# Four edits at the seams of a four-layer cross-attention kernel: interleaved row maxima, re-spread loads, an on-chip copy of Q rows, and sums of two tiles on TensorE

## The reference, cut to what matters

```python
q = hidden_states @ Wq                       # 2048 x 1024, 16 heads of 64
k = encoder_hidden_states @ Wk               # 1601 x 1024
v = encoder_hidden_states @ Wv
logits = jnp.einsum('bhqd,bhkd->bhqk', q, k) * scale
logits = logits + col_bias[None, None, :, :] # two masked columns pairs get -20
probs = jax.nn.softmax(logits, axis=-1)
out = jnp.einsum('bhqk,bhkd->bhqd', probs, v)
out = out @ Wo + bo + residual
```

## Time and profile before

| quantity | value |
|---|---|
| time, three runs | 4746.79, 4748.32, 4752.88 us; median 4748.32 us |
| time of the profiled execution | 4749.55 us, of which its span is 4747.40 us (2.15 us lie around the span) |
| busy share of the span | PE 97%, PEld 60%, DVE 67%, ACT 48%, POOL 55% |
| mean granted TensorE clock | 0.983 of full speed |
| Q phases | about 503 to 604 us, 2469 to 2543 us, 3603 to 3676 us |

### The profile page before, as it was taken

One profiled execution on the slowest core, in us unless ns is written; L12 is line 12 of the kernel. 1 busy time (PEld: TensorE's weight loads), 2 busy tenths in 40 slices (PEclk: granted clock), 3 DMA queues, 4 the chain that ended last, 5 costly groups with the idle time before them and its releaser, 6 DMA issues.

```text
span 4747.4 us, 55870 instructions
## 1 busy us (share of the span) xinstructions
PE 4584.1 (97%) x20473; PEld 2827.9 (60%) x20473; DVE 3192.8 (67%) x5093; ACT 2296.7 (48%) x4069; POOL 2621.8 (55%) x1266
## 2 busy tenths in 40 slices
PE   8999799999999989999989999999998999999999
PEld 7888565555555445555546655555555655555554
DVE  3321367777777778887846777777766777777777
ACT  3232355454444436666664555445454544454543
POOL 0000267887778500110126777887774777887775
PEclk9999899999999979999999999999999999999999
DMA  4564822221221021011134122211216122221210
GB/s 155 165 208 153 273 61 56 57 58 33 57 58 42 3 51 22 19 24 27 23 99 149 44 52 58 58 42 40 57 46 199 33 55 58 58 57 34 57 42 19
DMA packets 99522, 332.29 MB, mean 70 GB/s; under 512 B 13797, under 2 KB 32229, under 8 KB 87274
## 3 DMA queue, kind: packets, MB, share of 16 engines
q1 hardware_dynamic: 99248, 328.71, 25.5%
HBM read 193.15 MB, written 120.31 MB: 66 GB/s over the span
## 4 chain that ended last, share of the span: by engine, by line
PE 89%; DVE 6%; issue 3%; DMA 1%; ACT 1%; POOL 0%; SPq 0%; DVEq 0%; ACTq 0%
PE ST L890 13%; PE SS L871 12%; PE ST L891 12%; PE OA L901 12%; PE OB L901 11%; PE ST L1003 4%; PE OA L1011 4%; PE SS L922 4%; PE SS L989 3%; DVE mpart L1494 2%; PE SS L911 2%; DVE R L1510 1%; PE OB L989 1%; PE ST L937 1%; PE ST L939 1%
## 5 line engine op out<-in xcount | busy, mean ns | idle before, releaser
L774 POOL TENSOR_TENSOR acc<-acc,P 128x1024 f32<-128x1024 f32 x900 | 2153.6, 2424 | 617.7 <-DVE acc L1426 604.5
L1190 ACT ACTIVATE P<-ST 128x512 f32<-128x512 f32 (+1 forms) x2496 | 1465.5, 597 | 1297.8 <-PE ST L891 1150.3
L1402 DVE TENSOR_REDUCE mpart<-SS 128x1 f32<-128x400 f32 (+1 forms) x3072 | 1627.8, 569 | 640.7 <-PE SS L871 562.9
L871 PE MATMUL SS<-KS,QS 68*128 68x400 f32 (+1 forms) x3072 | 1042.7, 373 | 43.0 <-DMA QS<-q_parts 29.8
L890 PE MATMUL ST<-QX,KX 128*128 128x512 f32 (+1 forms) x2496 | 1033.1, 414 | 1.9 <-ACT stw L1097 1.8
L891 PE MATMUL ST<-QS,KS 69*128 69x512 f32 (+1 forms) x2496 | 989.2, 396 | 0.0
L871 PEld LDWEIGHTS SS<-KS,QS 68*128 68x128 f32 x3072 | 585.1, 191 | 260.2 <-DVE mpart L1402 52.9
L890 PEld LDWEIGHTS ST<-QX,KX 128*128 128x128 f32 (+1 forms) x2496 | 463.0, 185 | 387.9 <-issue 284.8
L901 PE MATMUL OA<-P,Vp 128*64 128x512 f32 (+1 forms) x2496 | 658.3, 606 | 0.0
L901 PE MATMUL OB<-P,Vp 128*64 128x512 f32 (+1 forms) x2496 | 641.3, 592 | 0.0
L1261 ACT ACTIVATE PG<-ST 128x512 f32<-128x512 f32 (+1 forms) x832 | 429.3, 614 | 245.6 <-PE ST L1003 245.3
(11 more groups left out here) (232 smaller groups left out, 4355.7 us busy)
## 6 DMA issues: line engine op xcount, KB each, us to landing
q_parts<-stq SPq DMA_DIRECT2D x96, 512.0 KB, 3.8
QX<-q_parts SPq DMA_DIRECT2D x96, 512.0 KB, 11.5
KX<-k_parts SPq DMA_DIRECT2D x48, 801.0 KB, 9.1
QS<-q_parts SPq DMA_DIRECT2D x48, 512.0 KB
v_tiles<-sv SPq DMA_DIRECT2D x24, 832.0 KB, 6.4
Vp<-v_tiles SPq DMA_DIRECT2D x24, 832.0 KB, 7.2
k_parts<-skh SPq DMA_DIRECT2D x48, 400.5 KB, 4.7
k_parts<-skl SPq DMA_DIRECT2D x48, 400.5 KB, 5.9
```

The source lines that it names most:

```text
L774: gp.tensor_tensor(out, out, P[0:k, slot(H, t), q, :], ALU.add).then_inc(pool_a, 1)
L871: pe.matmul(SS[at % 3][:, 0:w], QS[H % 3][0:SROWS, qt * 128:(qt + 1) * 128], KS[H % 3][0:SROWS, o:o + w], start=True, stop=True).then_inc( ...
L1190: act.activation(P[0:k, slot(H, t), j, :], ST[n % 3][0:k, :], ACT.Exp, scale=SCALE).then_inc(act_p, 1)
L1402: dve.tensor_reduce(mpart[H % 2][:, i // len(KCH), c:c + 1], SS[RING_AT["s", H, i] % 3][:, 0:w], AX.X, ALU.max).then_inc(dve_ss, 1)
```

## The change

Line numbers in the profile of before are those of before; the order listings below of the change carry its own.

1. `S_FROM, S_TO` go from 10, 26 to 8, 24, so `ROW_ITEM` goes from 27 to 25. Two of an item's four score tiles are issued between its two halves (`ct` = 0 and 1) and two behind it, no longer all four behind it.
2. The loads that SyncE issued in one block before the first Q phase (`first_loads`) are spread between the Q stores or moved behind them. The loads of `wqh` and `wql` are issued two K projections earlier. At the start of the first Q phase TensorE waits for each bank by itself.
3. QS of the first head is no longer read back from `q_parts`: after each of the first four stores SyncE copies the 64 rows from `stq` to `QS`, inside SBUF, in pieces of 512 queries.
4. In head 15 VectorE adds tiles 1, 2, 5 to 10, GpSimd tiles 3 and 4, and `sums` takes tiles 11 and 12 straight from P with eight more matmuls by ones. `sums` of head 15 is issued before the last `values`, and ScalarE's `take_z` before its `take_o`.

```diff
-S_FROM, S_TO = 10, 26
+S_FROM, S_TO = 8, 24
...
 def dve_tiles(h):
-    return range(1, 3 if h + 1 < HEADS else KT)
+    return [1, 2] if h + 1 < HEADS else [1, 2] + list(range(5, KT - 2))
 def pool_tiles(h):
-    return range(dve_tiles(h)[-1] + 1, KT)
+    return list(range(3, KT if h + 1 < HEADS else 5))
...
+        def s_loaded(H):
+            return sum(16 * (7 if i % HEADS == 0 else 4) for i in range(H % 3, H + 1, 3))
...
-                    if n == BIG * PAIRS - 2:
+                    if n == BIG * PAIRS - 4:
                         sp.wait_ge(d_sv, 64 * QUADS)
                         load_wq(0, 0)
                         load_wq(0, 1)
...
                 for q in range(QITEMS):
...
-                    if q == 6:
+                    if q < JQ:
+                        sp.dma_start(words(QS[H0 % 3][0:D, q * 512:q * 512 + 512]), words(stq[q][0:D, 1, :]))\
+                            .then_inc(d_s[H0 % 3], 16)
+                    if q == 10 and l == 0:
+                        load_head_kx(0)
+                    if q == 13:
                         wait_q(H0)
-                        for H in range(H0, H0 + 2):
-                            load_head_q(H)
-                            load_head_qx(H)
-                    if q == 12:
-                        wait_q(H0 + 2)
-                        load_head_q(H0 + 2)
+                        load_head_qx(H0)
+                    if q == 16 and l == 0:
+                        load_head_k(1)
+                        load_head_b(1)
+                    if q == 18:
+                        load_head_q(H0 + 1)
+                    if q == 22 and l == 0:
+                        load_v(0)
                     if q == ROW_ITEM:
                         max_row(H0)
+                if l == 0:
+                    load_head_k(2)
+                    load_head_b(2)
+                wait_q(H0 + 2)
+                load_head_q(H0 + 2)
+                if l == 0:
+                    load_head_kx(1)
+                load_head_qx(H0 + 1)
...
             def sums(H):
-                wait_added(pe, H, KT - 1)
+                own = range(KT - 2, KT) if H % HEADS == HEADS - 1 else []
+                wait_added(pe, H, KT - 1 - len(own))
...
-                        last = pe.matmul(SS[at % 3][64 * e:64 * e + 64, :], ones[:, 0:64], acc[H % 2][:, 2 * c + e, :],
-                                         start=True, stop=True)
+                        bank, j = SS[at % 3][64 * e:64 * e + 64, :], 2 * c + e
+                        last = pe.matmul(bank, ones[:, 0:64], acc[H % 2][:, j, :], start=True, stop=not own)
+                        for t in own:
+                            k = rows_of(t)
+                            last = pe.matmul(bank, ones[0:k, 0:64], P[0:k, slot(H, t), j, :],
+                                             start=False, stop=t == KT - 1)
...
-                    last.then_inc(pe_q, 1)
-                    for i in q_tiles(q):
-                        s_tile(H0, i)
+                        if ct == CT - 1:
+                            last.then_inc(pe_q, 1)
+                        tiles = q_tiles(q)
+                        for i in tiles[len(tiles) * ct // CT:len(tiles) * (ct + 1) // CT]:
+                            s_tile(H0, i)
...
                     pe.wait_ge(act_p, HU * H + JQ * (PV[g][-1] + 1))
+                    if h + 1 == HEADS and g + 1 == STEPS:
+                        sums(H)
                     for t in PV[g]:
                         values(H, t)
...
             def end(l):
-                sums(l * HEADS + HEADS - 1)
```

More of the change, by code:

```diff
@@ L593, in max_row @@
                              words(mrow[:, :])).then_inc(d_m, 16)
-            def first_loads():
-                for H in range(3):
-                    load_head_k(H)
-                    load_head_b(H)
-                for H in range(2):
-                    load_head_kx(H)
-                for n in range(2):
-                    load_v(n)
-                    load_wo(n)
             def q_phase(l):
                 H0, n0 = l * HEADS, l * PAIRS
+                if l == 0:
+                    load_head_k(0)
+                    load_head_b(0)
                 if l == 2:
@@ L759, in head @@
                     if H % HEADS > 0 and t in (7, 8, 9, 10):
-                        if H % HEADS + 1 < HEADS:
-                            gp.wait_ge(pool_a, first + 2 * (t - 3))
+                        gp.wait_ge(pool_a, first + 2 * min(t - 3, len(pool_tiles(H % HEADS))))
                         divide(H - 1, t - 7)
@@ L934, in q_phase @@
                         pe.wait_ge(act_qw, n - 2)
+                    if l == 0 and q < 4:
+                        for b in (q,) if q < 3 else range(3, 8):
+                            wait_bank(pe, 8 + max(i for i in range(len(BEFORE)) if i % 8 == b))
                     bank = ST[q % 3][:, :]
@@ L1221, in q_phase @@
                         act.wait_ge(d_q[i], q_stored(l, q - NSTG))
+                        if q == NSTG:
+                            act.wait_ge(d_s[H0 % 3], s_loaded(H0))
                     copy(stq[i][:, 1, :], ST[q % 3][:, :]).then_inc(act_qh, 1)
@@ L1236, in head @@
                     wait_stored(l, range(5))
+                if h + 1 == HEADS:
+                    take_z(H)
                 take_o(H)
@@ L1297, in _ @@
                     head(l, h)
-                take_z(l * HEADS + HEADS - 1)
                 if l == 0:
```

17 lines of the change are left out of this document (12 added, 5 removed).

## The result

The changed kernel takes 4719.56 us (median of 4, 4717.39 to 4720.07), the kernel before beside it 4748.89 us. The ratio is 0.9932 with a 95% interval of 0.992 to 0.9944: faster by 0.7%, some 29 us. I had forecast 4697 us with a range of 4680 to 4711. The direction was right, and the gain is little more than half of what I summed.

What follows compares the result with a forecast made beforehand. TensorE was 89% of the chain, with gains only where it stalls or is paced, a latency pattern in the Q phases. Phases 29.1 + 15.9 + 14.2 less 7.5 for ends gave 51.7 us: 4697 us, range 4680 to 4711.

Steps and rivals of the forecast that it cites:

- An item falls from 2.70 to 2.12 us: Q phases: with score tiles in pairs between the halves no bank wait is left; new phase 44.4 us to first scores.
- The rival that the stores set the pace: Q phases: stores slow the phases until ScalarE finds no free staging buffer; slower than before, 4790 us, chance 0.02.
- The stall shrinks from 5.05 to some 0.2 us, and the clock ... stays up: Second Q phase: copied QS rows arrive at 2483.1, so TensorE hardly waits before the maxima; phase saves 15.9 us.
- In the second phase 1.4 us of that was a wait ... it goes, because the row of maxima is now sent two items earlier: Second Q phase, ahead of the first scores: a wait of 1.4 us goes because the row is sent earlier.
- The first phase: First Q phase: barrier at 513, maxima start at 524 not 551.28 (bounds 519 to 530); phase gains 29.1 us.
- The row of maxima was late: First Q phase: the row, landing in 1.8 to 3.5 us, is late by 0 to 6 us; 3 taken.
- Cost: 2.5 us at each of three ends: Ends of the big layers: reciprocals start 2.4 us later; 7.5 us lost in all, bounds 0 and 5.
- my 0.7 us: End of a big layer: the sums begin 0.7 us later because of the new chain of additions.
- hide beside them, nearly: End of a big layer: tile 12's values and the output copies nearly hide beside the reciprocals.
- The bound of 5 us in the forecast: End of a big layer: upper bound of the cost, if GpSimd and VectorE hold each other up once more.
- The two adders do hold each other up: End of a big layer: tile 5's first half waits for GpSimd's last addition; without it an end costs 1.1 us less.
- The chance of 0.15 for a worse queue (4710 us): Q phases: barrier 518, first-phase maxima at 530, row 6 us late, other phases' copy 2 us late; chance 0.15.

Runs made afterwards that it cites:

- experiment 3: The kernel before with only two score tiles issued behind each half of a Q item, instead of four behind the whole item: 4728.01 us, ratio 0.995.
- experiment 5: The kernel of experiment 1 with the four copies into QS issued ahead of the stores, each waiting for ScalarE's upper part only: 4689.08 us, ratio 0.9868.
- experiment 7: The kernel of experiment 1 with the banks turned in the second Q phase and the row of maxima sent ahead of item 25's store: 4702.41 us.
- experiment 2: The changed kernel with the last tile's values moved back ahead of the sums and ScalarE's output copy before the sums: 4711.40 us, ratio 0.9917.
- experiment 4: The changed kernel with the load of the Q weights back at its old place behind the last K store: 4719.49 us, ratio 0.9932.
- experiment 10: The kernel of experiment 9 with the load of the Q weights back at its old place: 4682.32 us, ratio 0.9855.
- experiment 1: The changed kernel with the whole edit to the last head undone (old ends): 4704.49 us, ratio 0.9899.
- experiment 9: The kernel of experiment 1 plus copies into QS by VectorE, experiment 7's edits, and only tile 12 of the last head summed by TensorE: 4678.45 us.

## Why the prediction was right in its direction and wrong in its size

**What bounds the kernel, and the pairs: right.** "An item falls from 2.70 to 2.12 us" was measured as 2.14, in the changed kernel and alone in experiment 3. The rival that the stores set the pace did not occur: in none of the three Q phases does ScalarE wait for a free staging buffer.

**"The stall shrinks from 5.05 to some 0.2 us, and the clock ... stays up": this step failed.** The stalls were 2.98 and 3.24 us. They have two parts. First, I let the last copy go out 0.4 us behind a store that I took from the old spacing of 1.25 us. With copies in between, the third and the fourth store took 2.17 and 1.94 us to issue with their copies, the fourth copy left 12.1 us behind the first Q matmul where I had 10.2, and the first tile began 3.75 us later (I had 4.2): it stood 15.9 us behind the first Q matmul, not 14.4. SyncE issues without a break from 2455.42 on, so the queue of issues was late, not the transfers. Experiment 5 takes the copies out of that queue, away from the stores and from GpSimd, and the stall is gone. Second, I misread where the old maxima began: behind item 10, not item 9. Between 2468.70 and the old stall stand 22 matmuls on L937, two an item, so eleven items. TensorE therefore comes to the first pair 12.9 us behind the first Q matmul and not 14.2, and even a copy on my time would have left a stall of 1.5 us.

The stall of 3 us also brought the lower level of the clock, 1.2 GHz, for some microseconds behind it: from first to last tile 34.9 us in both phases instead of the 33.3 and 33.5 of experiment 5. In the second phase the late copy (1.5 us), the clock (1.6) and the bank below (1.4) make 4.5 of the 4.7 us that are missing by the ledger, in the third the late copy and the clock (1.5 each) make 3.0 of 3.5. In experiment 5 these two phases gave 16.0 and 15.5 us where I had 15.9 and 14.2. That the second agrees is in part luck: its first tile comes at 12.7 us, 1.7 earlier than I had it, and this covers the wait for the bank, which stays.

**"In the second phase 1.4 us of that was a wait ... it goes, because the row of maxima is now sent two items earlier": wrong cause.** The wait stayed at 1.38 us. Experiment 7 shows that it is the bank: layer 2's first scores fall on the bank of the last Q item, and those of the other layers do not. The row named the wait `ACT stw`, and I read past it.

**The first phase: the total nearly right, its parts not.** Forecast 29.1 us, measured 26.6. The preparation ended 1.9 us later than before (504.70 against 502.84). The barrier fell at 516.60 and not at 513, so the maxima started at 528.45 and not at 524, close to the 530 of my bounds. Both numbers differ between executions of the same code: in experiment 2, which is the changed kernel up to here, the preparation ended at 502.24, the barrier fell at 512.93 and the maxima began at 525.23. These 3 us are more than the 2.5 that the phase lacks, so its shortfall can't be put down to a cause. The stretch behind it took 49.0 us, where I had 50.4. The early load of the weights by itself was worth nothing in this kernel (experiment 4): it moved 10 us of waiting from one place to the next. It is worth some 4 us once the copies are off the queue (experiment 10). The row of maxima was late by 1.6 us (forecast 3, between 0 and 6), and it landed after 6.9 us, twice my upper value.

**"Cost: 2.5 us at each of three ends": the term that was most mis-sized.** It cost 7.3, 6.6 and 5.6 us. The start of the sums was right and even without my 0.7 us: the lead there is 30.49 us (3588.11 less 3557.62) against 30.6 in the layer. What follows, up to the first division, is 5.4 us at each of the three ends. It is made of three things that the forecast did not have or had too small. Twelve matmuls cost 2.7 us to the reciprocals (experiment 2) where I had 1.7 for the first bank's six. In the kernel before, the matmuls into the two halves of a bank start together and pass side by side; now those of the second half start 0.9 us behind (1622.85 and 1623.73 at the first end of experiment 4), so that eight steps of 0.43 us pass where it was two, and not six. The pause of 2 us ahead of them brought the clock to 0.50, which is 1.7 us more (6.12 against 4.45 in experiment 4, with the same pause and no fall). And the values of tile 12 with the copy of the output did not "hide beside them, nearly": the first division began 4.50 us behind the reciprocals' start instead of 3.49. That is 2.7 + 1.7 + 1.0 = 5.4 us. The other 1.9, 1.2 and 0.2 us are lost behind the divisions and are not shown to come from the edit. At the second end 1.2 us are the output matmuls, which took 10.14 us instead of 8.93 with more of them at the lower clock; but with the old ends of experiment 1 they took 8.6, 9.9 and 9.4 us, and at an end where the clock did not fall (the second of experiments 4 and 9) 7.3.

The bound of 5 us in the forecast was made for the hop over GpSimd, and this turned out to cost nothing at the end.

The two adders do hold each other up as the forecast said. The wait of 7.03 us for `acc` ahead of tile 5 is only the order of the chain; what shows it is the row behind: the two additions of tile 5 take 4.42 us where those of tile 2 take 2.35, and the first of them stands beside GpSimd's last addition. The Trainium skill (SBUF — State Buffer, "Who interferes with whom") has the rule, and this row agrees with it; only it was no part of the path.

The chance of 0.15 for a worse queue (4710 us) was in the right direction: its barrier of 518, its maxima at 530 and a copy 2 us late came near (516.60, 528.45, 1.5), but it too had the ends at 2.5. Both failed steps lack the clock. I charged its fall in the first phase, where I expected a long stall, and nowhere for stalls of 2 and 3 us: 1.6 and 1.5 us in the phases and 1.7 at each end are 8.2 of the 22.6 us.

## What to carry to other kernels

A DMA that is short and urgent should have its turn ahead of long ones on the issuing queue, or be done by an engine that has nothing to do; price its issue slot from rows in which the queue is as full as it will be. When work is moved onto an engine at a seam, look in the rows for what follows a pause of TensorE of like length, and count such a pause twice, once as itself and once as matmuls at 1.2 GHz behind it (here 1.5 to 1.7 us for pauses of 2 to 3 us, not every time); prefer an order in which work that is ready fills the pause. Taking one wait away is worth only the distance to the next one that ends there: try it together with the edit that moves the next one, since experiments 4 and 10 give 0 and some 4 us for the same line.

## What the runs showed of the hardware that was not expected

A pause of TensorE of 2.0 us was enough to see the granted clock fall to 0.50, at all three ends of the changed kernel (1.99 to 2.02 us) and at one of three in experiment 4 (1.98 us), whose other two ends (2.03 and 2.04 us) kept 1.00 through the sums. Pauses that differ by a few hundredths of a microsecond fell on both sides, and 1.7 us hang on it each time. Two microseconds are no threshold either: in the group layer of the changed kernel TensorE pauses 14 times for 1.42 to 1.46 us, and behind three of these the granted clock reads 0.50 to 0.58 (windows of 3 us from 1882, 2107 and 2292), while a stall of 2.58 us in experiment 4 was followed by no fall. The Trainium skill (TensorE: Matmul & The Clock Gate, "What's actually happening") says that the number of matmuls that run at the lower clock is not the same from run to run of one kernel. Here it is not the same from end to end within one run of experiment 4.

An 8 KB transfer landed 6.9 us after its issue while the DMA share was 1.03 (570.50 to 577.40), where it had taken 1.8 us at the median before; sending it 1.1 us behind VectorE's write in experiment 7, and no longer 2.5 us, brought 0.7 us of that back. It was not tried on a queue of its own.
